# One load per step in the weight-maximum stage, and two more places for the weight-quantisation step in the attention loop

## The reference

```python
def layer(x, ...):
    xn = layernorm(x)                                   # 4 x 4096 x 1024
    s = deltanet(xn, conv_w, Wq, Wk, Wv, Wb, Wg, norm_w, Wo)
    g = silu(ffn(xn, gate_w, up_w, down_w, s_in, s_in_down))
    return x + s * g

def deltanet(...):
    h = silu(conv4(xn)); q, k = l2norm(h @ Wq), l2norm(h @ Wk); v = h @ Wv
    beta = sigmoid(h @ Wb)
    # per head, chunks of 64 tokens, state S carried from chunk to chunk
    A = tril(kb @ kc.T, -1); U = solve(I + A, v * b - kb @ S)
    o = q @ S + tril(q @ k.T) @ U;  S = S + k.T @ U
    return (rmsnorm(o) * norm_w * silu(h @ Wg)) @ Wo

def fake_quant(w, gs):                    # gs = 448 * 6 / max(abs(w)) for a weight
    amax = max(abs(block of 16))          # one value for 16 elements
    sc8 = float8(min(amax / 6 * gs, 448)); dq = sc8 / gs
    return sign(w) * nearest_fp4(min(abs(w) / dq, 6)) * dq
ffn = quant_linear(silu(quant_linear(x, gate)) * quant_linear(x, up), down)
```

## Time and profile before

| | us |
|---|---|
| median of 3 runs (lowest, highest) | 11055.25 (11046.82, 11065.81) |
| profiled execution | 11074.4 |
| its span, slowest core (core 3) | 11072.9 |
| spans of the 8 cores | 11015.6 to 11072.9 |
| DVE busy | 5270.9 (48%) |
| PE busy | 2562.5 (23%) |
| POOL busy, ACT busy | 1297.5 (12%), 861.0 (8%) |

### The profile page before, as it was taken

The page is one execution under the profiler, slowest core; times in us unless marked ns, Lnnn a source line. Parts: engine busy times, 40 slices in busy tenths (PEclk is TensorE's granted clock), DMA queues, the critical chain, the costliest instruction groups (busy, mean ns, idle before and its releaser), DMA issues.

```text
span 11072.9 us, 55481 instructions; the slowest of 8 cores (11015.6 to 11072.9 us)
## 1 busy us (share of the span) xinstructions
PE 2562.5 (23%) x11776; PEld 1199.0 (11%) x11776; DVE 5270.9 (48%) x8637; ACT 861.0 (8%) x1745; POOL 1297.5 (12%) x1124
## 2 busy tenths in 40 slices
PE   0000012222222222222222222333200323232336
PEld 0000001111111111111111111111100101111112
DVE  2445264444444444444444444444455666566622
ACT  0000001010011001100110011000000001000100
POOL 0000001111111111111111111000011111221200
PEclk9999985555555555555555555555555666666667
DMA  3221300100010000000100000000000000000033
GB/s 93 69 73 49 83 20 22 28 22 20 20 28 22 21 20 28 22 21 20 28 22 21 20 27 22 12 12 12 13 20 19 26 24 8 24 9 23 10 101 116
DMA packets 496217, 345.97 MB, mean 31 GB/s; under 512 B 393734, under 2 KB 393868, under 8 KB 495884
## 3 DMA queue, kind: packets, MB, share of 16 engines
q1 hardware_dynamic: 201356, 271.06, 7.8%
q10 hardware_dynamic: 294528, 71.37, 3.1%
HBM read 202.81 MB, written 93.33 MB: 27 GB/s over the span
## 4 chain that ended last, share of the span: by engine, by line
DVE 42%; PE 15%; DMA 11%; issue 8%; POOLq 7%; ACT 5%; DVEq 4%; POOL 3%; SPq 2%; ACTq 2%
POOLq L217 6%; DVE s_ub L1281 4%; DVEq L217 4%; PE p_A L1274 4%; DVE s_wq L590 4%; PE p_A L845 2%; SPq L198 2%; DVE s_q L756 2%; DMA s_qrd<-wrd_scratch 2%; ACTq L198 2%; PE p_A L1091 2%; DVE s_pw L1231 1%; DVE s_wq L605 1%; DVE s_wq L599 1%; DVE s_wq L596 1%
## 5 line engine op out<-in xcount | busy, mean ns | idle before, releaser
L802 PE MATMUL p_A<-s_wgc,s_xqT 128*128 128x512 bf16 x1024 | 361.1, 530 | 1978.4 <-DMA s_xqT<-s_hqb 644.7
L1281 DVE SCALAR_TENSOR_TENSOR s_ub<-p_A,s_ub 64x1024 bf16<-64x1024 f32 x384 | 469.3, 1222 | 493.8 <-PE p_A L1274 493.8
L1023 PE MATMUL p_A<-s_Wq,s_hT 128*128 128x512 bf16 x256 | 129.2, 505 | 2325.2 <-ACT s_hT L1017 2325.2
L586 DVE TENSOR_SCALAR s_wq<-s_qsg 128x512 f32<-128x512 f32 x192 | 82.0, 427 | 976.3 <-ACT s_qsg L584 970.5
L579 POOL TENSOR_TENSOR s_wq<-s_wsrc,s_qrd 128x512 f32<-128x512 f32 x192 | 202.9, 1057 | 2501.2 <-PE p_B L623 2202.8
L590 DVE SCALAR_TENSOR_TENSOR s_wq<-s_qsg,s_wq 128x512 f32<-128x512 f32 x576 | 398.8, 692 | 45.1 <-issue 2.6
L610 POOL TENSOR_TENSOR s_wq<-s_wq,s_qdq 128x512 f32<-128x512 f32 x192 | 202.8, 1056 | 1832.8 <-DVE s_wq L605 1832.8
L623 PE MATMUL p_B<-s_id,s_xnb 128*128 128x128 bf16 x768 | 99.1, 271 | 1318.5 <-POOL s_xnb L613 803.1
L802 PEld LDWEIGHTS p_A<-s_wgc,s_xqT 128*128 128x128 bf16 x1024 | 126.7, 128 | 2212.7 <-issue 2182.0
L629 ACT CAST s_xnb<-p_B 128x512 bf16<-128x512 f32 x192 | 112.1, 584 | 3218.7 <-PE p_B L623 3218.7
L1274 PE MATMUL p_A<-s_ub,s_pw 64*64 64x256 bf16 x1024 | 263.5, 410 | 378.8 <-DVE s_ub L1281 378.8
(11 more groups left out here) (221 smaller groups left out, 7638.9 us busy)
## 6 DMA issues: line engine op xcount, KB each, us to landing
s_wsrc<-gate_w SPq DMA_DIRECT2D x80, 256.0 KB
s_wsrc<-up_w SPq DMA_DIRECT2D x80, 256.0 KB
s_wsrc<-down_w SPq DMA_DIRECT2D x80, 256.0 KB
s_xt<-x_seq SPq DMA_DIRECT2D x32, 512.0 KB
o_woA<-s_q SPq DMA_DIRECT2D x32, 512.0 KB
o_woB<-s_q SPq DMA_DIRECT2D x32, 512.0 KB
s_xt<-x_own SPq DMA_DIRECT2D x32, 512.0 KB
hq_scratch<-s_hqb SPq DMA_DIRECT2D x64, 256.0 KB
```

The costliest lines, as they stand in the source:

```text
L802: em.op(t, lambda e, ch=ch, tt=tt, hf=hf: e.matmul(out=ts["p_A"][:, hf * 512:(hf + 1) * 512], lhsT=ts["s_xqT"][:, ch * 2048 + tt * 128: ch ...
L1281: em.op(v, lambda e, sgn=sgn: e.scalar_tensor_tensor(out=ts["s_ub"][hb, :], in0=ts["p_A"][hb, :], scalar=sgn, in1=ts["s_ub"][hb, :], op0=A ...
```

## The change

In stage 2 the pair task is replaced by a task for one piece of 128x512 (`emit_wamax1`): one load, one block maximum of 512 columns, one maximum over its 32 results, the fold, one store. Four buffers take turns, each with its own semaphore (`wa` to `wd`). There are 64 tasks for a weight in place of 32, so the list has 207 entries, 6 or 7 for a tile. In stage 3 `qstep` is called at two more places: between the cast of v and the gate's matmuls, and behind the copy L1150, ahead of the stores to `o_woA` and `o_woB`. Waits of SP in `emit_wladder`, `emit_wbounce` and `emit_wload` name the new semaphores.

```diff
-def emit_wamax_pair(em, ts, srcA, srcB, sheetA, sheetB, par):
+def emit_wamax1(em, ts, src, sheet, slot):
     v, s = "vector", "sync"
...
+    slot_ap = (ts["s_wsrc"][:], ts["s_wq1"][:], ts["s_wq3"][:],
+               ts["s_qsg"][:, 0:512])[slot]
+    grp = (ts["s_qam"], ts["s_qs8"], ts["s_qdq"], ts["s_qrd"])[slot]
+    sem = ("wa", "wb", "wc", "wd")[slot]
     em.wait(s, (sem,))
-    em.dma("qs", slotA, srcA)
-    em.dma("qs", slotB, srcB)
+    em.dma("qs", slot_ap, src)
     em.wait(v, ("qs",))
     em.op(v, lambda e: e.tensor_reduce(
-        out=grp[:, 0:32], in_=q3v(slotA, 32), axis=AX.X,
+        out=grp[:, 0:32], in_=q3v(slot_ap, 32), axis=AX.X,
         op=ALU.max, apply_absolute_value=True))
+    em.drain(v)
     em.op(v, lambda e: e.tensor_reduce(
-        out=grp[:, 32:64], in_=q3v(slotB, 32), axis=AX.X,
-        op=ALU.max, apply_absolute_value=True))
-    em.drain(v)
-    em.op(v, lambda e: e.tensor_reduce(
-        out=glob, in_=grp[:, 0:64], axis=AX.X,
+        out=grp[:, 32:33], in_=grp[:, 0:32], axis=AX.X,
         op=ALU.max, apply_absolute_value=True))
     em.drain(v)
     em.op(v, lambda e: e.tensor_tensor(
         out=ts["s_gs"][:, 15:16], in0=ts["s_gs"][:, 15:16],
-        in1=glob, op=ALU.max), inc=sem)
+        in1=grp[:, 32:33], op=ALU.max), inc=sem)
     em.drain(v)
     em.wait(s, (sem,))
-    em.dma("qs", sheetA, grp[:, 0:32])
-    em.dma("qs", sheetB, grp[:, 32:64])
+    em.dma("qs", sheet, grp[:, 0:32])
@@ emit_wladder
-        em.wait(s, ("vv", "gg"))
+        em.wait(s, ("vv", "wa", "wb", "wc", "wd"))
@@ emit_wbounce
-    em.wait(s, ("vv", "gg"))
+    em.wait(s, ("wa", "wb", "wc", "wd"))
@@ emit_wload
-    em.wait(s, ("wa",))
+    em.wait(s, ("wa", "wb", "wc", "wd", "vv"))
@@ phase_a, the list of tasks (for gate and up; down alike)
-            amax_tasks.append(lambda W=W, mi=mi, pp=pp: emit_wamax_pair(
...
+            for h in range(2):
+                amax1(W, mi, pp, h)
@@ phase_a, behind the cast of v
         em.op(v, lambda e: e.tensor_copy(out=ts["s_v"][:], in_=ts["p_A"][:]), inc="vv")
+        qstep(8 * (tt + 1))
         em.wait(t, ("vv",))
```

More of the change, by code:

```diff
@@ L894, in phase_a, with amax1 @@
     amax_tasks = []
+    ns = [0]
+    def amax1(W, mi, pp, h):
+        sl = ns[0] % 4
+        ns[0] += 1
+        amax_tasks.append(lambda: emit_wamax1(
+            em, ts, W[pp * 128:(pp + 1) * 128, h * 512:(h + 1) * 512],
+            WSCh[mi, :, 64 * pp + 32 * h:64 * pp + 32 * (h + 1)], sl))
     for mi, (W, gcol) in enumerate(((GWh, 6), (UWh, 9))):
         for pp in range(32):
-            amax_tasks.append(lambda W=W, mi=mi, pp=pp: emit_wamax_pair(
[L898 to L902, removed]
+            for h in range(2):
+                amax1(W, mi, pp, h)
         amax_tasks.append(lambda gcol=gcol: emit_wbounce(em, ts, gcol))
@@ L907, in phase_a @@
     for rc in range(8):
[L908 to L915, removed]
+        for cp in range(8):
+            sl = ns[0] % 4
+            ns[0] += 1
+            amax_tasks.append(lambda rc=rc, cp=cp, sl=sl: emit_wamax1(
+                em, ts, DWh[rc * 128:(rc + 1) * 128, cp * 512:(cp + 1) * 512],
+                WSCh[2, :, 256 * rc + 32 * cp:256 * rc + 32 * (cp + 1)], sl))
     amax_tasks.append(lambda: emit_wbounce(em, ts, 12))
```

## The result

The changed kernel takes 11154.09 us (median of 8 runs, 11142.05 to 11161.09) against 11057.38 us (8 runs, 11041.68 to 11086.5): ratio 1.0086, 95% interval 1.0075 to 1.0097. It is slower, by 97 us; the forecast was +38. Its profiled span is 11159.3 us on core 4 (before 11072.9 on core 3).

A forecast was written before the change was run, and what follows sets the result against it. No engine fills the kernel; one serial chain of hand-overs bounds it. +189 (stage 2) and -151 (stage 3) give +38 us; the profiled 11112, adjusted to run medians, becomes 11093 us, own range 11070 to 11125, outer 11020 to 11165.

The forecast's parts named there:

- Term 1: Stage 2, single loads in place of pairs: waits +150.5, DVE busy +52, tiles' own loads 13 off; +189 us.
- four buffers would not run ahead: Stage 2: SP's order keeps each single a whole round trip; the opposite, about 10530 us, got chance 0.01.
- Terms 2 and 3: Stage 3, one chain of eight moved from the tile's end: -6.3 us a tile, 24 tiles, -151 us.
- Term 2: Stage 3, new call between v's cast and the gate: chunk starts later, +11.3 us a tile, bounds 6.0 and 14.8.
- Term 3: Stage 3, new call behind the copy, ahead of the stores: copy to conv 34.57 becomes 16.9, 17.6 us off a tile.
- the late store: Rival, stage 2: the store's landing ends DVE's wait, a single waits 3.86 us and not 3.5, +58, 11151 us; chance 0.14.
- the chain hidden by the gate: Rival, stage 3: the gate's matmuls hide the new chain, costing 8 us; -41 us, 11014 us; chance 0.14.
- The lone load's shorter wait: Rival, stage 2: a single waits 3.25 to 3.35 us and not 3.5; about 11063 us; chance 0.21.
- The serial path POOL, SP, load, POOL: Stage 3: claimed to limit a chain behind another to a cycle of 14.76 us, which matmuls don't shorten.
- The 2.0 us a transfer: Stage 2: fixed cost per transfer from the Trainium skill; 96 more round trips are 192 us.

The follow-up runs named there:

- e2: The kernel before with both new quantisation calls, stage 2 and semaphores as before: 10920 us, ratio 0.9875.
- e1: The changed kernel without the two new quantisation calls, singles only: 11287 us, ratio 1.0210.
- e11: The changed kernel with SP's wait ahead of a quantisation load naming wa alone, not five semaphores: 11106 us, ratio 1.0047.
- e5: The changed kernel without stage 2's stores of block maxima, the ladder reading a piece of the gate weight instead: 11051 us, one run.
- e3: The kernel before with only the new call between v's cast and the gate: 10985 us, ratio 0.9935.
- e7: The changed kernel with SP's load wait naming wa alone, and two buffer sets for quantisation loads, each with its semaphore: 10841 us, ratio 0.9806.
- e8: The changed kernel with SP's load wait naming wa alone, stage 2 loads issued four steps ahead, and load and store semaphores per buffer: 10674 us, ratio 0.9657.

## Why the prediction was right in its sign and short in its size

- **The bound**, a serial chain whose hand-overs add up, held: every edit to it showed in the time.
- **Term 1**, +189 us: measured +192. A single behind another waits 3.51 us on core 4 (3.38 to 3.51 over the cores; 3.5 forecast), one behind a cast 0.17. DVE's 1.17 us were 1.18 (307.30 to 308.48). That four buffers would not run ahead held. The parts were off by small errors that cancel. By the means over the cores, the waits grew by 152 us (150.5 forecast) and DVE's work by 54 (52), but the tiles' own loads gained 9 and not 13, the ladders' loads lost 7, and DVE's wait in the bounces, which was to stay as it was, fell by 12 (this last wait lies between 25 and 49 us from core to core, so its part may be chance).
- **Terms 2 and 3**, -151 us: the calls gave -136 (e2). Term 2 was +11.3 us a tile, measured +11.6 (29.6 against 18.0). Term 3 was 34.57 - 16.9, rightly 17.7 off, and measured 34.8 - 17.5 = 17.3. I read both from one tile, and what counts is a small difference of large numbers: -6.3 became -5.7.
- **The step that failed:** "The new names in the waits of the loads cost nothing: POOL's end of the chain, which SP waited for already, comes behind all of them." It is true that they have been reached, but not that they are free. SP takes 0.055 us for each between POOL's end and the issue, and the loop has this path 192 times: +34 us (e1, e2, e11). Four names by 0.055 by 192 would be 42, so some of these gaps are probably off the path; which ones, no run shows.
- **Sum:** +192 - 136 + 34 = +90 us against a time of +97.
- **The range held by luck.** The measured 11154 us lies outside the forecast's own range, 11070 to 11125. It is inside 11020 to 11165 because the upper end was set beyond the late store's 11151 us, and e5 rules that mechanism out. That 11154 is so near to 11151 is chance.
- **The rivals:** the late store (e5) and the chain hidden by the gate (e3) are out. The lone load's shorter wait, 3.25 to 3.35 us, is out too, though the core with the shortest waits comes near it with 3.38. The serial path POOL, SP, load, POOL was a limit, as argued: with a second set of buffers (e7) the loop falls by 261 us. But behind it the next limit is close, as the cycle of 13.6 us shows where 12.2 was expected.
- **A reading of the stretches:** 5322.5 us, 221.8 a tile, left out the last 9.7 us of tile 23; it is 222.2. Only the forecast of 215.5 us a tile rests on it; measured were 218.2.
- **The 2.0 us a transfer:** the Trainium skill ("DMA: Bandwidth & Descriptors", section "Anatomy of one DMA") gives them for transfers that GpSimd issues, and SP issues these. No term was worked out from them.

## What to carry to other kernels

More buffers brought almost nothing while one queue issued load, store, load, and waited for the consumer before each store; only behind a layer norm did they help. What helped was to issue the load of a later step ahead of the wait for this one, with semaphores that count each buffer's load and store alone (e8: 442 us of stage 2 less than in the changed kernel). Work moved out of a tile's end is worth what it no longer waits for, less what it waits for at its new place; read both from the chain of hand-overs, over many tiles. On a path that is walked hundreds of times, count the waits too, even those that are always satisfied, when they stand behind the one that is not.

## What was unexpected of the hardware

A wait on a semaphore that had already been reached took SP 0.055 us (0.08, 0.19 and 0.30 us from POOL's end to the load's issue with one, three and five names). The stores with rows of 128 B showed no landing time of their own in DVE's wait: taking them out shortened it by 0.47 us, about the 0.43 of their issue (one run, e5).
